# Register loads of TensorE in its waits, and unread products of the identity around two attentions

## The reference, cut to what matters

```
h = concat(tok(x), txt)                       # patch embedding
h = h + attention0(layernorm(h))              # 12 heads of 16
h = h + soft_moe(layernorm(h))                # 64 slots, each with its own 192-768-192 network
h = h + attention1(layernorm(h))              # one head of 192, rotary, causal
h = h + moe(layernorm(h))                     # 8 experts, top 2, 192-768-192
```

## Time and profile before

| | us |
|---|---|
| median of 3 runs | 910.83 (908.28 to 911.85) |
| the profiled execution, its own time | 912.18 |
| its span, first to last instruction | 910.2 |
| TensorE busy | 749.0 (82%) |
| DVE busy | 538.2 (59%) |
| ACT busy | 423.4 (47%) |
| POOL busy | 351.1 (39%) |

### The profile page before, as it was taken

The page is one execution under the profiler, slowest core; times in us unless marked ns, Lnnn a source line. Parts: engine busy times, 40 slices in busy tenths (PEclk is TensorE's granted clock), DMA queues, the critical chain, the costliest instruction groups (busy, mean ns, idle before and its releaser), DMA issues. The chain is left out here.

```text
span 910.2 us, 23578 instructions
## 1 busy us (share of the span) xinstructions
PE 749.0 (82%) x8514; PEld 639.4 (70%) x8514; DVE 538.2 (59%) x1461; ACT 423.4 (47%) x1072; POOL 351.1 (39%) x390
## 2 busy tenths in 40 slices
PE   3689999999988766556579999945299999999993
PEld 2577888888876544434457778733299999999993
DVE  1698878878772311111476777777455666566662
ACT  3666676766752311111114787573044444444441
POOL 1433444344321000000104778510336567666664
PEclk8799999999975987889859999965599999999997
DMA  9409200000016999999429000047258788888882
GB/s 245 133 12 414 100 1 3 1 3 2 3 61 207 385 427 426 426 426 423 148 99 395 27 3 26 27 124 188 70 190 240 237 248 251 246 238 245 233 215 31
DMA packets 55142, 163.31 MB, mean 179 GB/s; under 512 B 12256, under 2 KB 30338, under 8 KB 50688
## 3 DMA queue, kind: packets, MB, share of 16 engines
q1 hardware_dynamic: 43072, 147.48, 44.0%
q0 software_dynamic: 11968, 14.41, 8.8%
HBM read 107.04 MB, written 12.16 MB: 131 GB/s over the span
## 5 line engine op out<-in xcount | busy, mean ns | idle before, releaser
L2135 PE MATMUL psum<-x_x_hi,w_buf 128*128 128x256 f32 x558 | 126.5, 296 | 4.3 <-issue 2.6
L2070 DVE SCALAR_TENSOR_TENSOR x_h_lo<-psum,x_h_hi 128x256 fp32r<-128x256 f32 x186 | 78.6, 422 | 86.7 <-ACT x_h_hi L2031 85.8
L2031 ACT ACTIVATE x_h_hi<-psum 128x256 fp32r<-128x256 f32 x186 | 71.4, 384 | 123.0 <-PE psum L2154 115.7
L2151 PE MATMUL psum<-w_pairs,x_h_hi 128*128 x372 | 116.3, 350 | 0.0
L2135 PE MATMUL psum<-x_x_lo,w_buf 128*128 128x256 f32 x372 | 97.8, 284 | 0.0
L2135 PEld LDWEIGHTS psum<-x_x_hi,w_buf 128*128 128x128 f32 x558 | 92.7, 193 | 6.5 <-issue 4.6
L2154 PE MATMUL psum<-w_pairs,x_h_lo 128*128 x372 | 93.1, 250 | 0.0
L1993 POOL DMA_INDIRECT late<-xtab,idx x62 | 62.3, 1004 | 68.8 <-POOLq L1712 37.5
L549 POOL TENSOR_SCALAR a_u<-flat,a_mv 96x192 f32<-96x192 f32 x32 | 24.2, 757 | 126.3 <-DVE a_mv L743 126.3
L2135 PEld LDWEIGHTS psum<-x_x_lo,w_buf 128*128 128x128 f32 x372 | 71.3, 192 | 0.0
L2154 PEld LDWEIGHTS psum<-w_pairs,x_h_lo 128*128 128x128 f32 x372 | 70.8, 190 | 0.0
(11 more groups left out here) (277 smaller groups left out, 1955.0 us busy)
## 6 DMA issues: line engine op xcount, KB each, us to landing
flat<-in_slot_w SPq DMA_DIRECT2D x23, 2304.0 KB, 31.1
w_buf<-w_first SPq DMA_DIRECT2D x31, 768.0 KB
ring<-in_slot_w SPq DMA_DIRECT2D x8, 2304.0 KB, 30.5
w_buf<-w_hi_a SPq DMA_DIRECT2D x31, 384.0 KB
flat<-in_moe_w SPq DMA_DIRECT2D x1, 10752.0 KB, 29.3
flat<-in_x_patches SPq DMA_DIRECT2D x4, 1536.0 KB, 14.6
w_buf<-w_first SPq DMA_DIRECT2D x31, 192.0 KB
flat<-in_slot_w SPq DMA_DIRECT2D x4, 576.0 KB, 33.9
```

Of the source, the lines that this page charges most:

```text
L2031: act.activation(h_hi[:, k, :], b_f[k % NF1], ACT.Relu).then_inc(s_hh, 1)
L2070: v.scalar_tensor_tensor(h_lo[:, k, :], b_f[k % NF1], 0.0, h_hi[:, k, :].bitcast(F32), ALU.max, ALU.subtract).then_inc(s_hl, 1)
L2135: mm = pe.matmul(b_f[k % NF1], w[0:rows, part, cols], x[0:rows, u % 2, c, :], start=(m == 0), stop=(m == len(terms) - 1))
L2151: pe.matmul(bank, h_hi[:, k, part], g.w_pairs[:, :, k, bass.ds(e, 1), :].rearrange("p two a d -> p two (a d)"), start=(k == 0), stop=False)
```

## The change

Three kinds of edit. (1) `keep_warm` multiplies the 128x128 identity by itself into a PSUM bank that nobody reads then; 28 such products stand in the closing order of the first attention, 11 in the loop of L1623 (odd batches from 11 on) and 6 behind L1694. (2) `te` is computed right behind `ctiles`, ahead of the tokens' places. (3) TensorE's register loads: 8 ahead of the list (was 5), 7 behind it (was 6), and the other 16 (was 20) now ahead of the wait for `s_one` instead of behind it.

```diff
-TE_EARLY, TE_LISTS = 5, 11
+TE_EARLY, TE_LISTS = 8, 15
...
                 of_chunk(t, 3 * CH + 2, gather)
+            pe.wait_ge(s_qs, B)
+            pe.wait_ge(s_ks, B)
+            keep_warm(pe, g, 1, 8)
             values(B - 2)
...
             last_product(B - 3)
+            pe.wait_ge(s_res, B - 1)
+            keep_warm(pe, g, 2, 3)
             output(B - 1)
             transposes(CLOSE + 1)
             gather(END - 2)
             last_product(B - 2)
+            keep_warm(pe, g, 2, 2)
             transposes(CLOSE + 2)
+            keep_warm(pe, g, 2, 3)
             last_product(B - 1)
             turn_dispatch(END - 1)
+            keep_warm(pe, g, 2, 4)
             transpose_logits(END)
             turn_combine(END - 1)
+            keep_warm(pe, g, 2, 2)
             gather(END - 1)
+            keep_warm(pe, g, 2, 3)
             turn_dispatch(END)
+            keep_warm(pe, g, 2, 3)
             gather(END)
             turn_combine(END)
...
                     pe.wait_ge(s_cres, b - NB + 1)
+                if b >= B // 3 and b % 2:
+                    keep_warm(pe, g, 6)
...
             mm.then_inc(s_csp, 1)
+            keep_warm(pe, g, 6, 6)
...
+            link(v.tensor_tensor(tge[:, :, :], wide(iota[:, 0:NTB], NE),
+                                 ctiles.unsqueeze(1).broadcast_to([128, NTB, NE]), ALU.is_ge))
+            link(v.tensor_reduce(tef[:, :], tge[:, :, :], AX.X, ALU.add))
+            v.tensor_scalar(g.te[:, :], tef[:, :], float(NE - 1), None, ALU.min).then_inc(s_te, 1)
+            v.tensor_scalar(g.te_less[:, :], tef[:, :], float(-NE), None, ALU.add)
             link(v.tensor_tensor(shift, ctiles, tiles, ALU.subtract))
...
+def keep_warm(pe, g, bank=7, n=1):
+    for _ in range(n):
+        pe.matmul(g.ps[:, bank, 0:128], g.ident[:, :], g.ident[:, :], start=True, stop=True)
...
         def _(pe):
-            pe.wait_ge(s_one, 2)
-
             for i in range(TE_LISTS, NTB):
                 pe.reg_load(g.expert_regs[i], g.te[0:1, i:i + 1])
+
+            pe.wait_ge(s_one, 2)
```

More of the change, by code:

```diff
@@ L1876, in columns @@
                 return x[:, :, :].rearrange("p k b -> p (k b)")[:, PART * q:PART * q + PART].unsqueeze(1).broadcast_to([T, n, PART])
[L1878 to L1882, removed]
             for q in range(NP):
```

## The result

| kernel | us, median (lowest to highest) | executions | ratio to before, 95% interval |
|---|---|---|---|
| before | 910.83 (908.28 to 912.0) | 5 | |
| after | 902.09 (900.43 to 903.84) | 5 | 0.992 [0.9896, 0.9944] |

The change gains 8.7 us between the medians and 7.3 by the ratio; its interval is 0.6 to 1.0%. The forecast was 895.0, a gain of 15.8. The profiled execution of after took 900.43 us, its span is 898.5 and its mean granted clock 0.911; the forecast for such an execution was 896.4.

The account below looks back on a forecast made before the run. It saw different bounds by stretch: TensorE's slow-clock chain, transfers in the slot networks, DVE in the loop, TensorE in routing and tiles. 912.18 - 6.1 - 0.0 - 9.7 = 896.4, less 1.35: 895.0 us; range 888 to 904.

Parts of the forecast that it names:

- Part 3: Routing and tile start: earlier te and moved register loads start list 2.7 us and transposes 7.0 us earlier, 9.7 together.
- the 0.895 us taken: Routing: the median time assumed for each of the eight register loads ahead of the list, done by 621.2.
- the 0.3 given back to DVE's split of the weights: First tile: DVE's eight pieces delay the split behind them, cutting the transposes' gain from 7.3 to 7.0 us.
- The bound "0.7 + 5 = 5.9": Routing and tile start: lower limit of the register-load gain if loads are slow in both places, 5.9 us.
- a rival: Routing and tile start: register loads slower where they now lie, gain 5.9 us, time 898.8; chance 8 in 100.
- Part 1: End of the first attention: 28 products keep TensorE's clock high, so it ends 6.1 us earlier.
- the rival of a falling clock: End of the first attention: the clock falls all the same, about +1 there, time 902; chance 15 in 100.
- Part 2: Ahead of the second attention: 17 products cost little and the faster start is given back; 0.0 us in sum.
- the bound of 4.1: Loop of L1623: cost in us of the eleven products if none were hidden; 0.3 was taken.
- the bound of 1.4: Behind L1694: six products at the low clock take 3.2 us in a wait of 1.77, so 1.4 late.
- the ramp's 4.2 us: Second attention's pipeline start: high clock saves about 4.2 us, lost waiting for the expert weights to land; about 0.3 left.
- the marks named ahead: Signs across the kernel: right if clock 1.00 from 264 into the slot networks; wrong if 0.50 between 264 and 284.

Follow-up runs that it names:

- part 3 alone: Before with only te computed early and TensorE's register loads moved, no identity products: 902.34 us, ratio 0.9929.
- before_again4: The unchanged kernel of before, executed once more for its trace: 906.62 us, one execution.
- later_only: Before with only the later 20 of the 28 identity products at the end of the first attention: 905.58 us, ratio 0.9963.
- best2: no_loop_early without the first eight of the 28 products in the first attention: 896.10 us, ratio 0.9815.
- no_loop_early: After without the 11 loop products and with most of the expert weights requested at the start of the block: 896.34 us, ratio 0.9855.
- no_loop: After without the 11 identity products in the loop of L1623, the six behind it kept: 897.77 us, ratio 0.987.
- att0_only: Before with only the 28 identity products at the end of the first attention: 908.09 us, ratio 0.9995.
- att0_again: The kernel of att0_only, executed once more for its trace: 908.51 us, one execution.
- half_loop: After with the 11 loop products cut from 128 to 64 columns: 902.68 us, one execution.
- early_w: After with the expert weights in three transfers, two of them issued at the start of the block: 900.33 us, ratio 0.9909.

## Why the prediction was right and where it failed

The sign and the range held; the size did not. 8.7 us were gained by the medians, 7.3 by the ratio, and 15.8 forecast. That the range held says little for parts 1 and 2: the register loads alone bring 902.34.

**Part 3, right.** -2.6 and -7.2 against -2.7 and -7.0, in every kernel that has it. The list waits for DVE, the transposes for POOL, as forecast. Two details were off. The early loads were faster than the 0.895 us taken: 0.303 in the median, one of 1.468, at a DMA share of 0.64 where the loads of before had 0.96. And the 0.3 given back to DVE's split of the weights did not appear: from the first transposes to the first product of the tiles it is 2.55 us in both. In the timed runs part 3 alone gives 6.1 us between the medians, and 3.9 to 9.0 by the interval of the ratio, less than the 9.8 of its trace; on top of the 28 products it gives 9.6. The three us between the first two are not accounted for: R repeats to 0.1 us in every trace, so they should lie in the stages that move or in the executions of before that it was compared with, and of this kernel one execution was traced. The bound "0.7 + 5 = 5.9" is 5.7 as printed; only a rival hangs on it.

**Part 1, right mechanism, sized too large.** The clock stayed at 1.00 from 38 us to 283.8, so the rival of a falling clock did not occur (the fall at 283.8 just ahead of the slot networks lasted 3.4 us). The Trainium skill had spoken for it: "TensorE: Matmul & The Clock Gate", Part 4 (PE-mode transpose), says that transposes do not count as work for the clock. One execution of before doesn't fit that rule. Timeline of TensorE in before_again4, between the fall of its clock at 261.5 and the rise at 264.9 (L1002 and L953 are transposes):

```profile
260.98 0.79 PE L1017 MATMUL psum<-ring 96*32 96x96 f32 x24 [1.88 <-DVE flat L739]
261.70 2.16 PE L1002 MATMUL psum<-ident,ring 96*96 96x96 f32 x12
263.65 0.53 PE L953 MATMUL psum<-ident,a_u 96*96 96x96 f32 x2
```

The clock came back behind a stretch in which 2.3 us of 3.4 were transposes. It is one execution, and the other 1.1 us were products.

Of the 6.1 us the trace shows 4.3. Up to the last gather the sum holds: it starts 3.8 us earlier behind the first transposes (255.69 to 251.85), where 4.2 were forecast. Then 1.9 more were to come, 1.2 of which did (1.59 instead of 2.78). Ahead of the next block turn_combine loses instead of gaining: the standstill of 1.02 us inside L1081. It stands, 0.70 to 1.05 us long, in all nine traces with the 28 products and in no other. No wait of the program stands there. The traces hold a likely cause, the loading of instructions: in all nine a 16 KB packet of the queue that the page calls q8 instruction begins 1.1 to 1.3 us ahead of the last product before the standstill (in after at 279.81, landed at 280.79), and TensorE goes on 1.3 to 1.5 us behind its landing (282.22). With the eight products or none the same packet begins 2.4 to 2.9 us ahead of the last turn_combine. It is not shown: in later_only and best2 the packet is as close (1.4 and 1.1) and nothing stands still; their programs have eight of the added products fewer ahead of that place. Besides, the step took the traced execution of before for the rule, where in three of six the clock comes back by itself, for 3.4 to 6.8 us.

**Part 2, the step that failed.** The prediction put it: "Eleven products go into the loop of L1623 ... DVE sets the pace and has three pairs of banks to run on. ... I take 0.3." They cost 4.4 us, even a little over the bound of 4.1 that it gave for the case that nothing is hidden. Two things were wrong. First the price: 0.72 us in the loop at the low clock, not 0.53, because the instructions of 192 columns from which 0.53 was scaled are no measure of 128 columns: halving the product's columns takes only 0.10 away. Second the cover: it was read as a sum over the stretch and written off to buffers. Read per pair of batches, gives 12.5 / 10 = 1.25 us for DVE and 10.82 / 10 = 1.08 for TensorE, 0.17 of spare time for a product of 0.53: even at its own price the loop had to pass to TensorE, at 0.36 x 11 = 4 us. That this comes so near to the 4.4 is partly chance: in after the eight instructions of a pair take 0.89 and not 1.08, and the product 0.72 and not 0.53, and both sums are 1.61. Three pairs of banks smooth out single late products, not one in every pair. The clock did not help: it was 0.50 through the whole loop. The six products cost 0.8 (3.34 against 2.55), within the bound of 1.4 that was named for the low clock and not taken.
That the ramp's 4.2 us would be given back at the landing was right, and with it the waits: ACT ahead of its step 8, TensorE behind ACT. What was missed is that the wait does more than use up the lead: the clock drops again behind it for 3.4 us, so P became 0.8 longer instead of 0.3 shorter; in later_only, where the wait came without that drop, it is 0.2 shorter.

In sum, for the profiled execution: +6.0 instead of 0.0 in part 2, -4.3 instead of -6.1 in part 1, -9.8 instead of -9.7 in part 3, and 3.6 us that vary on their own. Of the marks named ahead, the list, the tiles, the last turn_combine (280.85 for "about 281") and ACT's wait came as the right ones, and the clock up to 283.8, 0.2 us inside the stretch in which a fall was to count as wrong. The loop was not among the marks, and that was the place.

## What to carry to other kernels

Register loads and other work that depends on nothing late belong ahead of a wait, not behind it: that part was certain, and the same in each trace that has it. A filler product needs a wait of its own size at its own place, in every round of the loop, at the price of the low clock; in a loop count the two engines' time per round, not per stretch. Before a slow start is sped up, move the transfer that lands under it, otherwise the lead ends in a wait and may cost the clock as well; in the traces this was worth up to 3.6 us, in the timed runs 1.4 to 1.8, which the noise doesn't separate from nothing.

## What the runs showed of the hardware

- An f32 product of the 128x128 identity takes 0.25 us from start to start at the high clock (four in a row) and 0.45 at the low one (six in a row), but 0.72 where it alternates with other products at the low clock; with 64 columns instead of 128 it is 0.62.
- With the same program on TensorE the clock rises up to 9.3 us earlier or later (0.8 and 10.1 us behind the first transposes, no_loop_early and no_loop), and in before it comes back for 3.4 to 6.8 us in a busy stretch in three of six traces. One trace is no measure of an edit that works through the clock.
- In the four traces in which ACT waited 1.9 to 2.8 us for the expert weights behind an early rise (after, att0_only, att0_again, half_loop), 3.4 us at 0.50 followed; in later_only it waited 1.67 us and none followed, nor where ACT did not wait (no_loop_early, early_w, best2).
- TensorE's register loads take 0.302 us in the median, 0.303 for the eight of after at a DMA share of 0.64 with one of 1.47; the five of before at a share of 0.96 took 0.48 to 1.19 each. Other traces show the same two cases.
